# Two-layer graph and attention network on one core: causal mask of the diagonal scores moved from TensorE to VectorE, part of the last stage's normalisation moved into the attention, first graph attention rows loaded earlier

## The reference, cut to what matters

```python
# graph attention: softmax over all nodes, bias added in front
logits = f1 + f2.T
coefs = softmax(leaky_relu(logits, negative_slope=0.2) + adj_bias_mat, axis=-1)
vals = coefs @ h + bias
# attention: 4 heads (d = 64), 4 experts a head: each expert has its own queries, keys and values are shared
q = einsum('bnsd,neod->bneso', sx, wq)
causal = where(tril(ones((s, s), bool)), 0.0, -inf)
scores = einsum('bnesd,bntd->bnest', q, k) * d ** 0.5 + causal
att = softmax(scores, axis=-1)
qkv = einsum('bnest,bntd->bnesd', att, v)
...                                    # gate over the experts, mixed = sum of the weighed experts
hn = layernorm(mixed + resid, ln_g, ln_b)
hx = relu(where(pm, 0.0, fx @ fc1_w.T + fc1_b))
hx = layernorm(where(pm, 0.0, hx @ fc2_w.T + fc2_b) + fx, fnorm_g, fnorm_b)
fg = softmax(fout @ fgate_w.T, axis=-1)
out = fout.reshape(b, s, nh, d) * fg[..., None]
```

## Time and profile before

| | us |
|---|---|
| median of 3 runs | 3293.67 |
| lowest, highest | 3292.46, 3295.69 |
| the profiled execution | 3291.56 |
| its span in the trace | 3289.8 |
| stages up to the end of the graph attention's preparation | 0 to 651 |
| graph attention | 651 to 1018 |
| attention, preparation | 1018 to 1071 |
| attention | 1071 to 3150 |
| last stage | 3150 to 3290 |

### The profile page before, as it was taken

One profiled execution on the slowest core, in us unless ns is written; L12 is line 12 of the kernel. 1 busy time (PEld: TensorE's weight loads), 2 busy tenths in 40 slices (PEclk: granted clock), 3 DMA queues, 4 the chain that ended last, 5 costly groups with the idle time before them and its releaser, 6 DMA issues. The chain is left out here.

```text
span 3289.8 us, 45640 instructions
## 1 busy us (share of the span) xinstructions
PE 2946.1 (90%) x17338; PEld 1824.7 (55%) x17338; DVE 1934.4 (59%) x3686; ACT 1255.6 (38%) x1714; POOL 1728.1 (53%) x946
## 2 busy tenths in 40 slices
PE   7999897859999799999999999878999999999953
PEld 3457565548887455555555555445555555555532
DVE  3555664387762466666565662156666566575566
ACT  2242221255553233444444444323434444444423
POOL 0030020233330256778889899735687879888014
PEclk9999887979999799999999999889999999999976
DMA  9971200099990000000000000000000000000001
GB/s 391 423 263 49 64 1 0 35 293 277 270 214 17 3 1 1 1 1 1 1 1 1 1 4 1 1 1 1 1 1 1 1 1 1 1 1 1 1 9 35
DMA packets 63623, 195.20 MB, mean 59 GB/s; under 512 B 8243, under 2 KB 25009, under 8 KB 53426
## 3 DMA queue, kind: packets, MB, share of 16 engines
q1 hardware_dynamic: 38658, 147.98, 11.7%
q0 software_dynamic: 24752, 44.31, 7.5%
HBM read 188.86 MB, written 3.41 MB: 58 GB/s over the span
## 5 line engine op out<-in xcount | busy, mean ns | idle before, releaser
L2136 POOL TENSOR_TENSOR at_acc<-at_acc,at_pt 128x1024 f32<-128x1024 f32 (+1 forms) x628 | 1335.0, 2126 | 233.6 <-ACT at_pt L1879 161.5
L1879 ACT ACTIVATE at_pt<-at_psR 128x1024 f32<-128x1024 f32 (+3 forms) x776 | 700.4, 942 | 936.5 <-PE at_psR L1786 584.2
L1953 DVE TENSOR_REDUCE at_mx<-at_psR 128x2 f32<-128x1024 f32 x576 | 701.6, 1224 | 413.9 <-PE at_psR L1770 411.9
L1804 PE MATMUL at_psO<-at_pt,v 128*64 128x512 f32 (+3 forms) x3104 | 701.6, 573 | 0.4 <-ACT at_pt L1879 0.3
L1770 PE MATMUL at_psR<-at_khi,at_qhi 64*128 64x512 f32 (+3 forms) x1568 | 350.6, 443 | 53.1 <-DVE at_mx L1953 25.5
L1804 PEld LDWEIGHTS at_psO<-at_pt,v 128*64 128x64 f32 x3104 | 191.1, 138 | 328.2 <-issue 227.6
L1770 PEld LDWEIGHTS at_psR<-at_khi,at_qhi 64*128 64x128 f32 x1568 | 154.7, 187 | 326.8 <-issue 296.0
L1783 PE MATMUL at_psR<-at_qhi,at_klo 64*128 64x512 f32 (+2 forms) x1552 | 311.2, 395 | 24.5 <-ACT at_pt L1879 14.5
L1316 PE MATMUL ga_acc<-h,ga_ring 128*128 128x257 f32 (+1 forms) x1352 | 306.9, 388 | 28.9 <-ACT ga_ring L1210 25.2
L1316 PEld LDWEIGHTS ga_acc<-h,ga_ring 128*128 128x128 f32 (+1 forms) x1352 | 259.5, 194 | 74.5 <-ACT ga_ring L1210 32.9
L1783 PE MATMUL at_psR<-at_qlo,at_khi 64*128 64x512 f32 (+2 forms) x1552 | 295.7, 375 | 0.0
(11 more groups left out here) (338 smaller groups left out, 3618.0 us busy)
## 6 DMA issues: line engine op xcount, KB each, us to landing
gc_rows<-in_adj SPq DMA_DIRECT2D x26, 1664.0 KB, 17.4
ga_rows<-in_adj SPq DMA_DIRECT2D x26, 1664.0 KB, 10.3
ga_ring<-in_adjT POOLq DMA_DIRECT2D x78, 512.0 KB, 23.7
gc_cols<-in_adjT SPq DMA_DIRECT2D x26, 1024.0 KB, 14.8
gc_ring<-in_adjT SPq DMA_DIRECT2D x26, 512.0 KB, 8.0
gc_ring<-in_adjT SPq DMA_DIRECT2D x13, 256.0 KB, 2.8
ga_ring<-in_adjT POOLq DMA_DIRECT2D x13, 256.0 KB, 11.1
out_x<-X SPq DMA_DIRECT2D x6, 512.0 KB
```

Source lines behind the costliest of these rows:

```text
L1804: ins = pe.matmul(columns(psO[lanes[l], :], g), v1[:, t, (2 * hp + l) * D:(2 * hp + l + 1) * D], packed(pt[:, g % PTS, l, 0:w], g), start= ...
L1879: act.activation(pt[:, g % PTS, :, 0:w], psR[:, slot_of["score", g] % SLOTS, :, 0:w], ACT.Exp).then_inc(e_ready, 1)
L1953: dve.tensor_reduce(mx[:, u % 2, :, s, c:c + 1].rearrange("p l o -> p (l o)"), got[:, :, 0:w], AX.X, ALU.max).then_inc(p1_read, 1)
L2136: pool.tensor_tensor(to, to, got, ALU.add).then_inc(added, 1)
```

## The change

**The mask.** `isel` and the bf16 `hide_col` go; `hide_col` becomes one 128x128 float triangle. The four products of a diagonal group (L1792) go, so the group's semaphore comes with the last product of L1786. DVE gets `hide_later_keys(g)`: it waits for that semaphore and adds the triangle onto the group's square in PSUM, in place, for both lanes at once (twice for a group of block 0, which has two experts). ACT's exponential of a diagonal group waits for this as well. In DVE's order the two additions stand behind half 0 of the row maxima, `finish_queries` and `sum_of_experts` (for units of 5 steps or more) and ahead of half 1. PE no longer waits for the masks at the stage's start, and DVE for four instructions of POOL instead of eight.

**Normalisation in the attention.** The buffer of reciprocal roots becomes part of `FfnWeights`. In units 50 and 51 DVE does, one operation a step behind its additions, what the last stage did for blocks 0 to 4: the variances in step 0, the reciprocal in step 4, then ten operations of 128x1024. ACT does one root for it in the third step of unit 50. The last stage computes roots for the last two blocks alone, starts turns of blocks 0 to 4 without a wait, and normalises block 5 in iteration 3 and block 6 in iteration 4.

**Rows ahead.** The buffers and semaphores of `ga_rows` are opened around both graph attention stages, and SP issues the loads of row tiles 0 and 1 in `stage_gat_prepare`, behind its four weight loads.

```diff
@@ stage_gat_prepare
                 sp.dma_start(b_sb[:, :], row_on_all(bias)).then_inc(w_loaded, 16)
+                for i in range(2):
+                    gat_rows.load(sp, adj, i)
@@
+class GatRows:
+    def __init__(self, m):
+        self.rows = m.sb("ga_rows", [P, 2, NP])
+        self.loaded = [m.sem(f"ga_rows_loaded{k}") for k in range(2)]
+
+    def load(self, sp, adj, i):
+        b, s = ROW_TILES[i]
+        t = GAT_BLOCKS[b][0] // P + s
+        sp.dma_start(self.rows[:, i % 2, :], adj[t * P:(t + 1) * P, :]).then_inc(self.loaded[i % 2], 16)
@@ stage_gat
-                for i, (b, s) in enumerate(ROW_TILES):
-                    if i >= 2:
-                        sp.wait_ge(row_max, i - 1)
-                    t = BLOCKS[b][0] // P + s
-                    sp.dma_start(rows[:, i % 2, :], adj[t * P:(t + 1) * P, :]).then_inc(rows_loaded[i % 2], 16)
+                for i in range(2, len(ROW_TILES)):
+                    sp.wait_ge(row_max, i - 1)
+                    gat_rows.load(sp, adj, i)
@@ stage_attention, buffers
-        isel = m.sb("at_isel", [P, 2, P], BF16)
-        hide_col = m.sb("at_hide_col", [P, 2, P], BF16)
+        hide_col = m.sb("at_hide_col", [P, P])
@@ stage_attention, TensorE
                     for l in range(2):
                         ins = pe.matmul(packed(psR[:, slot, l, 0:w], g), ones_r[lanes[l], :],
-                                        columns(nm[lanes[l], u % 2, :], g), start=False, stop=not diag)
-                    if diag:
-                        for x in range(0, w, w // EXPERTS[b]):
-                            for h in range(2):
-                                for l in range(2):
-                                    ins = pe.matmul(psR[:, slot, l, x:x + P], isel[lanes[l], h, :],
-                                                    hide_col[lanes[l], h, :], start=False,
-                                                    stop=h == 1 and x + w // EXPERTS[b] == w)
+                                        columns(nm[lanes[l], u % 2, :], g), start=False, stop=True)
-                pe.wait_ge(hides, 8)
@@ stage_attention, ScalarE
                 def exps(g):
                     u, t, off, w = GROUPS[g]
+                    if has_diagonal(g):
+                        act.wait_ge(hidden, DIAGONAL_UPTO[g])
                     act.wait_ge(s_full, g + 1)
@@
+                        if u == NU - 2 and k == 2:
+                            act.wait_ge(ffn_var, 1)
+                            act.activation(ffn.rstd[:, 0:er], ffn.rstd[:, 0:er], ACT.Sqrt).then_inc(ffn_std, 1)
@@ stage_attention, VectorE
-                dve.wait_ge(hides, 8)
+                dve.wait_ge(hides, 4)
+                def hide_later_keys(g):
+                    u, t, off, w = GROUPS[g]
+                    nx = EXPERTS[UNITS[u][1]]
+                    dve.wait_ge(s_full, g + 1)
+                    for x in range(0, w, w // nx):
+                        got = psR[:, slot_of["score", g] % SLOTS, :, x:x + P]
+                        ins = dve.tensor_tensor(got, got, hide_col[:, :].unsqueeze(1).broadcast_to([P, 2, P]), ALU.add)
+                    ins.then_inc(hidden, 1)
+                def normalise_early(step):
+                    rstd = ffn.rstd[:, 0:er]
+                    if step == 0:
+                        dve.tensor_scalar(rstd, hn_mv[:, 0:early, :, 1].rearrange("p t n -> p (t n)"), EPS2, None,
+                                          ALU.add).then_inc(ffn_var, 1)
+                    elif step == 4:
+                        dve.wait_ge(ffn_std, 1)
+                        link(dve.reciprocal(rstd, rstd))
+                    elif 5 <= step < 5 + 2 * EARLY_NORMS:
+                        b, scaling = divmod(step - 5, 2)
+                        v = hn[:, b * SUB:(b + 1) * SUB, :].rearrange("p t (n d) -> p (t n) d", d=D)
+                        by = (ffn.rstd[:, b * SUB * NH:(b + 1) * SUB * NH] if scaling else
+                              hn_mv[:, b * SUB:(b + 1) * SUB, :, 0].rearrange("p t n -> p (t n)"))
+                        link(dve.tensor_tensor(v, v, by.unsqueeze(2).broadcast_to([P, SUB * NH, D]),
+                                               ALU.mult if scaling else ALU.subtract))
@@
+                hide_later_keys(0)
+                hide_later_keys(1)
                 for u in range(NU):
                     for k in range(steps_of(u)):
                         for piece in max_pieces(u, k, 0):
@@
+                        for g in (FIRST[u] + 2 * k + 2, FIRST[u] + 2 * k + 3):
+                            if g < ng and has_diagonal(g):
+                                hide_later_keys(g)
                         for piece in max_pieces(u, k, 1):
                             row_max(u + 2, *piece)
@@
+                            normalise_early((u - NU + 2) * steps_of(u) + k)
@@ stage_attention, GpSimd
-                pool.memset(isel[:, :, :], 0.0).then_inc(hides, 1)
                 pool.memset(hide_row[:, :], 0.0).then_inc(hides, 1)
-                pool.memset(hide_col[:, :, :], 0.0).then_inc(hides, 1)
-                for e in range(2):
-                    pool.affine_select(out=isel[lanes[e], :, :], in_=isel[lanes[e], :, :], compare_op=ALU.not_equal, fill=1.0,
-                                       base=0, pattern=[[D, 2], [-1, P]], channel_multiplier=1).then_inc(hides, 1)
-                    pool.affine_select(out=hide_col[lanes[e], :, :], in_=hide_col[lanes[e], :, :], compare_op=ALU.is_ge,
-                                       fill=NEG, base=0, pattern=[[-D, 2], [1, P]], channel_multiplier=-1).then_inc(hides, 1)
+                pool.memset(hide_col[:, :], 0.0).then_inc(hides, 1)
+                pool.affine_select(out=hide_col[:, :], in_=hide_col[:, :], compare_op=ALU.is_ge, fill=NEG, base=0,
+                                   pattern=[[1, P]], channel_multiplier=-1).then_inc(hides, 1)
@@ stage_ffn
-                    pe.wait_ge(normed, b + 1)
+                    if b >= EARLY_NORMS:
+                        pe.wait_ge(normed, b - EARLY_NORMS + 1)
-                norm(0)
-                norm(1)
                 for b in range(NBLK):
                     mask_hidden(b)
-                    if b + 2 < NBLK:
+                    if EARLY_NORMS <= b + 2 < NBLK:
                         norm(b + 2)
```

More of the change, by code:

```diff
@@ L1132, in stage_gat @@
     BANKS = 7
-    ROW_TILES = [(b, s) for b in range(NBK) for s in range(BLOCKS[b][1] // P)]
     ROW_OF = {x: i for i, x in enumerate(ROW_TILES)}
@@ L1528, in max_pieces, with has_diagonal @@
     return [(CHUNKS_UPTO[u + 2] + i, *some[i]) for i in range(lo, hi)]
+def has_diagonal(g):
+    u, t, _, _ = GROUPS[g]
+    return t * P >= QBLOCKS[UNITS[u][1]][0]
+DIAGONAL_UPTO = [sum(has_diagonal(x) for x in range(g + 1)) for g in range(FIRST[NU])]
 def gate_pieces(u, k):
```

640 lines of the change are left out of this document (323 added, 317 removed).

## The result

The changed kernel takes 3318.14 us (median of 4 runs, 3317.39 to 3324.47) against 3293.07 us for the kernel before, measured beside it: ratio 1.0082, 95% interval 1.0070 to 1.0094, some 27 us slower. The forecast was 3291.0 with a range up to 3315: the kernel became slower where no clear change was forecast, and the time lies beyond the range.

A forecast was written before the change was run, and what follows sets the result against it. PE was taken as the bound in long units, waits in short ones. Terms -33 + 41 - 3.2 - 2.9 - 5.5 + 1 = -2.6 us against a median of 3293.67 gave 3291.0 us, range 3264 to 3315.

The forecast's parts named there:

- the saving on TensorE: Diagonal groups: removing the mask products saves 0.16 us for each of 208 sets, -33 us where PE is the bound.
- The price of the additions: Diagonal steps: VectorE's additions make exponentials, and so PSUM slots, late; +41 us, from +18 to +64.
- +8 and +1: Net terms: the mask in sum +8 us (-15 to +31), early normalisation in units 50 and 51 +1 us.
- The rival of 3314: Diagonal steps: VectorE's queue becomes the bound, give-back 64 us beside the saving of 33; 3314 us, chance 0.23.
- The prices by class: The +41 us split by units: experts 2 and 3 of blocks 3 to 5 9.6, block 2 8.4, block 1 10.4, others.
- the clock as a rival of its own: Short units: PE's longer stalls lower the granted clock, some 17 us on top of the forecast; 3308 us, chance 0.04.
- a point of decision of 0.44 us a diagonal step: VectorE as the bound: give-back per diagonal step (100 of them) from which it decides; beyond 0.50 a measurable loss.
- The addition itself: VectorE: 208 additions of 128x256 at 0.42 us each, with no stall charged for the busy POOL.
- Rows ahead: Graph attention: rows loaded earlier let ACT and DVE start sooner and shorten PE's idle time; -3.2 us (-3.8 to 0).
- Start of the attention: Attention's start: PE no longer waits for POOL's last mask piece, only for the constants; -2.9 us.
- Last stage: Last stage: the first turn starts at once and iteration 2 loses two operations; -5.5 us (-8 to -3).
- Units 50 and 51: Attention's units 50 and 51: early normalisation mostly fits VectorE's idle time, buffers soak up part; +1 us (0 to +3).

The follow-up runs named there:

- e2: Changed kernel with no causal mask on the scores: no products, no additions, no ScalarE wait for them; 3272.05 us, ratio 0.9921.
- e1: Changed kernel with the mask back on TensorE as before; rows ahead and early normalisation stay; 3285.41 us, ratio 0.9966.
- e3: Changed kernel with the four mask products back on TensorE and VectorE's additions kept (of -1); 3318.84 us, ratio 1.0065.
- e9: e1 with TensorE's wait for the masks moved from the attention's start to ahead of the first scores; 3281.24 us, ratio 0.9958.
- e6: e1 with ScalarE's diagonal exponentials waiting for VectorE, which there only copies one column (128x1); 3305.52 us, ratio 1.0038.
- e8: Changed kernel with four more TensorE products, adding zero, for each diagonal group of blocks 1 and 2; 3315.04 us, ratio 1.0064.
- e11: Changed kernel with TensorE doing one group's values ahead of half 1 of the first-pass products in diagonal steps; 3284.34 us, ratio 0.9970.

## Why the prediction was wrong

**The failed step: the saving on TensorE, wrong by three times.** The step "208 x 0.16 = **-33 us** where PE is the bound" took its condition from PE's busy share over long windows and not from the diagonal steps. The rows it priced the set from even held a wait of 0.22 us for ACT; a product that waits for a slot says that PE is not the bound there. The 20 waits for an exponential that the working counted were those of the scores alone; 11 more stood ahead of first-pass products. The count of starts was right (0.33 us a step are gone from PE), but the saving was about 11 us by e2 against e1, since the rest came back as slot waits.

**The price of the additions: too low, and what it rests on was additive only on paper.** I had +41 beside -33. e3 against e1 puts the additions at 33 us with the products in place, and the changed kernel against e2 at 1.6%, about 53 us, without them. Added and removed work lie in the same slot wait; the net is read from changed against e9: 1.0082 to 0.9958, 41 us, of which 3.5 are unit 51. The forecast had +8 and +1. The rival of 3314 held a saving of 33 and a give-back of 64, where 11 and 53 were measured: its sum came near by luck, though its mechanism, the chain through VectorE, is the one that e6 shows.

The mechanism in the working was the right one and is shown: the exponential late by the queue (0.54 us in the long unit, 1.2 in the short, for which 1.7 was forecast), its slot late, the first-pass product waiting. The prices by class are a give-back without the products, so they are compared with the changed kernel against e2. The twelve units of experts 2 and 3 of blocks 3 to 5 were priced at 9.6 us and cost 6.5; with the products' saving taken off (against e1) 3.7 are left, 0.2 of them in block 3. Block 2's experts 2 and 3 were priced at 8.4 and cost 13.8, block 1's at 10.4 and cost 14.7. The rest, unit 51 aside, was priced at 13 and cost 6. What the working lacked in the short units is, in part, the clock. Timeline of the changed kernel in block 1's last expert: a wait of 1.66 us for the slot, forecast in kind, and then, behind a second late exponential, eight products of values in 3.25 us:

```profile
1188.42 0.75 DVE L2346 TENSOR_TENSOR at_psR<-at_psR,at_hide_col 128x256 f32<-128x256 f32 x2
1188.88 1.73 ACT L2249 ACTIVATE at_pt<-at_psR 128x1024 f32<-128x1024 f32 x2 [4.07 <-DVE at_psR L2346]
...
1190.05 0.50 PE L2147 MATMUL at_psR<-at_khi,at_qhi 64*128 64x512 f32 x2 [1.66 <-ACT at_pt L2249]
...
1198.89 3.25 PE L2173 MATMUL at_psO<-at_pt,v 128*64 128x512 f32 x8
```

The kernel before needs 1.73 us in that place:

```profile
1200.36 1.73 PE L1804 MATMUL at_psO<-at_pt,v 128*64 128x512 f32 x8
```

I had the clock as a rival of its own with 0.04 and a price of 17 us on top of the forecast. It was no separate case: where it came, it came behind slot waits. For VectorE as the bound I had worked out a point of decision of 0.44 us a diagonal step, from 33 us saved and 10.6 from the other parts. With 11 us truly saved it was (11 + 10.6) / 100, 0.22 us a step, half of that. The measured give-back, 0.53 us a step against e2, is beyond both; in e6, where VectorE only answers, it is 0.24, which lies at that point.

**The addition itself: right.** 208 of mean 427 ns against 0.42, beside a busy POOL:

```profile
L2346 DVE TENSOR_TENSOR at_psR<-at_psR,at_hide_col 128x256 f32<-128x256 f32 x208 | 82.9, 427 | 36.6 <-PE at_psR L2162 34.5
```

None of them waited a whole GpSimd instruction, 2.37 us in the mean for an addition of 128x1024 in this trace. The Trainium skill, page "SBUF — State Buffer", section "SBUF: two separate sides", lets a DVE instruction with one SBUF input go free. The trace agrees: beside the busy POOL the 208 additions took 422 to 433 ns.

**Rows ahead: right.** -3.2 forecast, -4.3 in the changed kernel and -3.3 in e1. ACT's first leaky row to PE's spread, 14.81 us before, is 10.97:

```profile
648.66 6.03 ACT L1215 ACTIVATE ga_leaky<-f_all,f1c 128x3327 f32<-128x3327 f32 x2 [23.93 <-PEq L71]
...
659.63 1.22 PE L1317 MATMUL ga_psM<-ga_diag,ones 128*128 128x128 f32 x4 [12.66 <-DVE ga_diag L1243]
```

**Start of the attention: right.** -2.9 forecast, -2.7 found up to the first product; the wait of 5.47 is 2.62:

```profile
1065.58 1.13 PE L2102 MATMUL at_psX<-sxT,at_wk 128*128 128x512 f32 x2 [2.62 <-POOL at_onx L2552]
```

**Last stage: right.** -5.5 forecast, -4.8 in the changed kernel, -7.0 in e1. `fxT` starts 4.34 us after the table load that opens the stage (8.70 before, counted from 3150.64):

```profile
3183.05 1.28 ACT L1666 ACT_TABLE_LOAD   x1 [10.24 <-PEq L71]
...
3187.39 1.21 ACT L1632 ACTIVATE ff_fxT<-ff_psT,ff_lnb,ff_lng 128x1024 f32<-128x1024 f32 x1
```

**Units 50 and 51: right without the mask, too low with it.** In e1 both units are as long as before to 0.1 us. ACT's root, in the changed kernel:

```profile
3071.96 1.28 ACT L2285 ACT_TABLE_LOAD   x1
3073.25 0.27 ACT L2285 ACTIVATE ff_rstd<-ff_rstd 128x80 f32<-128x80 f32 x1
3073.54 1.28 ACT L2249 ACT_TABLE_LOAD   x1
3074.83 1.94 ACT L2249 ACTIVATE at_pt<-at_psR 128x1024 f32<-128x1024 f32 x2
```

From the first load to the exponential pass 2.87 us, which the stretch of 2.54 and the buffers cover. The Trainium skill, page "ScalarE: Activation LUTs", section "What ACT_TABLE_LOAD costs", puts some 2.7 us on one switch. The trace differs, and it decides here: two switches and the root took 2.87 us together. The overflow at unit 50's diagonal steps was in the working with 0.7 us and hidden by "the buffers soak up part"; what it delayed was not an addition of exponentials but `take_out`, which stands behind it in the queue, and PE behind that; the clock that fell behind PE's wait made it 3.5 us.

## What to carry to other kernels

An engine's busy share over a window does not tell that it is the bound in a given step: look for the slot waits in the very rows from which a removed instruction is priced, since the time of the instruction turns into a longer wait there. A step of another engine put between producer and consumer costs by the wait for that engine before it costs by its length: a copy of 149 ns in that place cost 20 to 24 us here, the real addition 33, and about the same length of work without the wait 5 to 8, hardly clear of noise. Where such a wait can't be avoided, give the waiting engine work that is ready: one group of values ahead brought 37 us. It made the moved mask level with the mask on TensorE, not better.

## What the runs showed of the hardware

TensorE's clock fell from 1.00 to the 0.50 level for some three microseconds behind a wait of 0.90 us, and did not in the same place with waits of 0.86 and 0.64 us when eight bf16 products a step more stood around them; a unit became 3.4 us shorter by having more to do. More products did not always keep the clock up: in e8 it was at 0.50 from 1160 to 1165 us, in block 1's third expert, which is 4.7 us longer than in e1. A wait of 1.06 us in a nine-step unit left the clock at 1.00 (unit length +0.5).

The same pattern of work did not always get the same clock. Behind the wait of 1.95 us in unit 51 it fell to 0.50 in the changed kernel and stayed at 1.00 in e8 and e11. The second expert's unit of block 3 was 3.2 us longer in some traces than in others with no edit that touches it, in both head pairs in e1 and in the second pair in e9; in e1 it had this window of 6 us:

```profile
1368.00:1374.00 6.00, 6.00 (x23) 3.14 (x22) 3.01 (x7) 0.46 (x2) 3.51 (x2) 0.52 0.00 0
```

With differences of 3 us from that alone, traces of single runs were compared here by unit, and sums by the timed ratios.
